# Two 128-square turns per node tile move from TensorE: the counts to transposing DMAs, the edge weights to VectorE in squares of 32 and a regrouped reload

## The reference

```python
h = relu(layernorm(x))
x1 = h @ W1 + b1                      # layer 0: 1024 -> 512, then 4 gated sums over the edges
for kk in range(4):                   #   norm = dis[src] * dis[dst], dis = max(deg, 1) ** -0.5
    out += segment_sum(norm * tanh(out[dst] @ gw[:512] + out[src] @ gw[512:] + gb) * out[src], dst)
x = x + concat([x1, out])
W = zeros(1024, 1024).at[src, dst].add(edge_weight)   # layer 1: the edge weights as a matrix
x = x + relu(layernorm(x)) @ W.T + bias
# layer 2: a GCN layer over the same edges; layer 3: an attention layer over the same edges
```

## Time and profile before

| | us |
|---|---|
| median of the runs | 975.7 |
| the profiled execution, its own time | 974.37 |
| its span, first to last instruction | 972.6 |
| TensorE busy | 955.2 |
| VectorE busy | 713.5 |
| ScalarE busy | 496.8 |
| GpSimd busy | 152.0 |

### The profile page before, as it was taken

One profiled execution on the slowest core, in us unless ns is written; L12 is line 12 of the kernel. 1 busy time (PEld: TensorE's weight loads), 2 busy tenths in 40 slices (PEclk: granted clock), 3 DMA queues, 4 the chain that ended last, 5 costly groups with the idle time before them and its releaser, 6 DMA issues.

```text
span 972.6 us, 14172 instructions
## 1 busy us (share of the span) xinstructions
PE 955.2 (98%) x5140; PEld 794.5 (82%) x5140; DVE 713.5 (73%) x1277; ACT 496.8 (51%) x768; POOL 152.0 (16%) x197
## 2 busy tenths in 40 slices
PE   5999999999999999999999999999999999999998
PEld 3888878888888888888888888888888888888887
DVE  7987798788788789558885162797856664967787
ACT  5778864554554557323334344444622323656654
POOL 3022410000000001132223000014210000333331
PEclk9999999999999999999999999999999999999999
DMA  7256491000000005453424400044952220201222
GB/s 258 88 194 230 127 209 68 0 24 0 0 22 0 0 0 119 76 172 131 129 87 126 162 1 1 1 55 116 224 126 77 82 106 0 88 22 66 86 87 82
DMA packets 28472, 83.73 MB, mean 86 GB/s; under 512 B 4696, under 2 KB 4892, under 8 KB 28272
## 3 DMA queue, kind: packets, MB, share of 16 engines
q1 hardware_dynamic: 17536, 53.48, 16.6%
q0 software_dynamic: 10880, 29.50, 12.9%
HBM read 54.65 MB, written 33.57 MB: 91 GB/s over the span
## 4 chain that ended last, share of the span: by engine, by line
PE 95%; DVE 1%; ACT 1%; DMA 1%; issue 1%; POOL 1%; SPq 0%; ACTq 0%; DVEq 0%; POOLq 0%
PE ps L659 22%; PE ps L2492 13%; PE ps L2467 10%; PE ps L2384 9%; PE ps L2386 9%; PE ps L2385 9%; PE ps L2440 5%; PE ps L2436 5%; PE ps L642 3%; PE ps L2307 2%; PE ps L2308 1%; PE ps L2309 1%; PE ps L2232 1%; PE ps L2235 1%; PE ps L2276 1%; PE ps L2503 1%
## 5 line engine op out<-in xcount | busy, mean ns | idle before, releaser
L2384 PE MATMUL ps<-g_hi,mask_hi 128*128 128x512 f32 x400 | 157.7, 394 | 0.2
L2386 PE MATMUL ps<-g_hi,mask_lo 128*128 128x512 f32 x400 | 155.9, 390 | 0.0
L2385 PE MATMUL ps<-g_lo,mask_hi 128*128 128x512 f32 x400 | 155.7, 389 | 0.0
L1232 ACT ACTIVATE mask<-ps,v 128x640 f32<-128x640 f32 x80 | 63.2, 793 | 95.7 <-PE ps L2386 49.1
L2492 PE MATMUL ps<-y_all,att_hi 128*128 128x512 f32 x380 | 103.6, 392 | 0.0
L2384 PEld LDWEIGHTS ps<-g_hi,mask_hi 128*128 128x128 f32 x400 | 75.1, 188 | 19.1 <-DVE mask_lo L1762 2.3
L2386 PEld LDWEIGHTS ps<-g_hi,mask_lo 128*128 128x128 f32 x400 | 75.1, 188 | 16.0
L2385 PEld LDWEIGHTS ps<-g_lo,mask_hi 128*128 128x128 f32 x400 | 75.1, 188 | 14.8
L2467 PE MATMUL ps<-w_hi,parts 128*128 128x512 f32 x280 | 86.7, 389 | 0.0
L659 PE MATMUL ps<-w,hT_hi 128*128 128x512 f32 x320 | 86.6, 392 | 0.0
L625 ACT ACTIVATE hT_hi<-ps 128x1024 fp32r<-128x1024 f32 x30 | 30.8, 1026 | 104.7 <-PE ps L642 104.6
(11 more groups left out here) (248 smaller groups left out, 1989.5 us busy)
## 6 DMA issues: line engine op xcount, KB each, us to landing
xin<-x_after SPq DMA_DIRECT2D x20, 512.0 KB, 3.4
x_after<-g POOLq DMA_DIRECT2D x20, 256.0 KB, 7.6
xres<-x_after POOLq DMA_DIRECT2D x10, 512.0 KB, 3.6
x_after<-xres POOLq DMA_DIRECT2D x10, 512.0 KB, 3.1
xin<-in_x SPq DMA_DIRECT2D x9, 512.0 KB, 3.7
x_after<-in_x SPq DMA_DIRECT2D x8, 512.0 KB
weight_rows<-weight_row POOLq DMA_DIRECT2D x8, 512.0 KB, 3.9
wt_raw<-weight_rows SPq DMA_DIRECT2D x4, 1024.0 KB, 20.5
```

Source lines behind the costliest of these rows:

```text
L1232: nc.scalar.activation(mask[k][:, :], U_ALL, ACT.Tanh, bias=v[:, s:s + 1]).then_inc(tanh_ready, 1)
L2384: nc.tensor.matmul(SUMS[dd], mask_hi[k][:, cols], g_hi[:, s, :], start=(s == 0), stop=False)
L2385: nc.tensor.matmul(SUMS[dd], mask_hi[k][:, cols], g_lo[:, s, :], start=False, stop=False)
L2386: last = nc.tensor.matmul(SUMS[dd], mask_lo[k][:, cols], g_hi[:, s, :], start=False, stop=(s == T - 1))
```

## The change

The counts of a tile `a` are turned by ten transposing DMAs of 128 x 128, issued from SP's queue straight from `countT` to `count_row` (`turn_counts`). SP's program reaches them three steps behind the load of `xin` (`TURN_LAG`), since the load of step `t` is issued early. ScalarE still passes over `count_row` to sum the degree (`sum_count_rows`), now in place and three groups behind the tile's last one, before two. The cast to `count_b` is gone, and so are both kinds of TensorE transposes.

The weights of a tile are turned by one VectorE instruction (`turn_weights`), which turns each square of 32 x 32 in itself. The squares then stand in the wrong place; the reload puts them right: `squares` takes 32 rows at four places, so 32 DMAs of 32 partitions with runs of 256 floats replace four DMAs of 128 partitions with runs of 1024 floats. What is left out of order is the order of the output's columns, which `residual` undoes by four instructions in place of one. The semaphore's targets follow (`Dense(1, 1, 1 + 2 * QUARTERS)`). Code for the case `whole == 0`, which these inputs do not enter, changes likewise and is left out below.

```diff
@@ -47,6 +47,7 @@
 FIRST_STEP = 2
+TURN_LAG = 3
 LATE_TILE = FIRST_STEP + 2
...
@@ -91,6 +92,9 @@
 EARLY = 3
+SQUARE = 32
+QUARTERS = P // SQUARE
+GEN_STORES = 16 * (1 + QUARTERS)
 TAIL = 3
...
@@ -378,7 +380,7 @@
-    dense = [Dense(0, 0, 1), Dense(1, 1, 2), Dense(2, 2, 4)]
+    dense = [Dense(0, 0, 1), Dense(1, 1, 1 + 2 * QUARTERS), Dense(2, 2, W2_LOAD + 1)]
...
@@ -534,6 +532,14 @@
         return bass.ds(t * P, P)
+
+    def by_quarter(row):
+
+        return row.rearrange("p (i s r) -> p s i r", i=QUARTERS, r=SQUARE)
+
+    def squares(rows_of, j):
+
+        return rows_of.rearrange("(i c) (j x) -> j c i x", c=SQUARE, j=QUARTERS)[j]
...
@@ -743,12 +749,6 @@
-    def load_weights(eng, d, dram):
-        for q in range(4):
-            eng.dma_start(W_PAIRS[d.n][q],
-                          dram[2 * q * P:(2 * q + 2) * P, :].rearrange("(k p) n -> p k n", p=P)
-                          ).then_inc(w_landed[q], 16)
-
     def settled(eng, semaphore, value):
...
@@ -762,6 +762,13 @@
             sp.dma_start(to[0:EDGE_ROWS, :, :], of.rearrange("(t p c) -> p t c", t=EDGE_TILES, c=EP)).then_inc(landed, 16)
+
+        def turn_counts(a):
+
+            sp.wait_ge(counts_copied, last_group(a) + 1)
+            sp.wait_ge(count_stored[a % 2], 16 * (a // 2))
+            for s in range(T):
+                sp.dma_start_transpose(count_row[a % 2][:, s * P:(s + 1) * P], countT[:, s, a * P:(a + 1) * P]).then_inc(count_transposed[a % 2], 16)
...
@@ -778,8 +785,15 @@
             sp.dma_start(x1_dram[(t - 2) * P:(t - 1) * P, :], x[(t - 2) * P:(t - 1) * P, :]).then_inc(rows_stored, 16)
+            for place in range(PER_STEP):
+                for a in tiles_behind(t - TURN_LAG, place, 0):
+                    turn_counts(a)
         sp.dma_start(x1_dram[(T - 2) * P:N, :], x[(T - 2) * P:N, :]).then_inc(rows_stored, 16)
         sp.dma_start(x1_dram[N:NP, :], x[0:NP - N, :]).then_inc(rows_stored, 16)
+        for t in range(T - TURN_LAG, T):
+            for place in range(PER_STEP):
+                for a in tiles_behind(t, place, 0):
+                    turn_counts(a)
...
@@ -804,7 +820,11 @@
         sp.dma_start(dis_dram.rearrange("(t p) -> p t", p=P), dis[:, 1, :], allow_slow_non_contiguous=True).then_inc(consts_landed, 16)
-        load_weights(sp, dense[1], wt_dram)
+        for q in range(4):
+            for k in (2 * q, 2 * q + 1):
+                for j in range(QUARTERS):
+                    sp.dma_start(wt_raw[SQUARE * j:SQUARE * (j + 1), k, :].rearrange("c (i x) -> c i x", i=QUARTERS),
+                                 squares(wt_dram[k * P:(k + 1) * P, :], j)).then_inc(w_landed[q], 16)
         with sp.Fori(0, GATES - 1) as r:
...
@@ -1074,17 +1092,10 @@
-        def take_weight_rows(a):
-
-            act.wait_ge(weights_transposed, a + 1)
-            act.wait_ge(weights_stored[a % 2], 16 * (a // 2))
-            nc.scalar.activation(weight_row[a % 2][:, :], ROWS, ACT.Copy).then_inc(weights_copied, 1)
-
-        def take_count_rows(a):
-
-            act.wait_ge(count_transposed, a + 1)
-            act.wait_ge(count_stored[a % 2], 16 * (a // 2))
-            nc.scalar.activation(count_row[a % 2][:, :], COUNT_ROWS, ACT.Copy,
+        def sum_count_rows(a):
+
+            act.wait_ge(count_transposed[a % 2], 16 * T * (a // 2 + 1))
+            nc.scalar.activation(count_row[a % 2][:, :], count_row[a % 2][:, :], ACT.Copy,
                                  accum_out=deg[:, a:a + 1]).then_inc(count_row_ready, 1)
...
@@ -1109,11 +1120,8 @@
                 take_cells(n)
-            for a in tiles_behind(t, place, 1):
-                if a < WT_TILES:
-                    take_weight_rows(a)
-            for a in tiles_behind(t, place, 2):
-                take_count_rows(a)
+            for a in tiles_behind(t, place, 3):
+                sum_count_rows(a)
...
@@ -1609,19 +1618,20 @@
-        def count_rows_of(a):
-
-            dve.wait_ge(counts_copied, last_group(a) + 1)
-            if a >= 2:
-                dve.wait_ge(count_transposed, a - 1)
-            nc.vector.tensor_copy(count_b[a % 2][:, :, :], countT[:, :, a * P:(a + 1) * P]).then_inc(count_b_ready, 1)
+        def turn_weights(a):
+
+            dve.wait_ge(weights_taken, min(last_group(a) + 1, WEIGHT_GROUPS))
+            dve.wait_ge(weights_stored[a % 2], 16 * (a // 2))
+            nc.vector.transpose(weight_row[a % 2][:, :].rearrange("p (j s r) -> p j s r", j=QUARTERS, r=SQUARE),
+                                weights_sd[:, :, a * P:(a + 1) * P].rearrange("p s (j c) -> p j s c", c=SQUARE)).then_inc(weights_copied, 1)
             for a in tiles_behind(t, place, 1):
-                count_rows_of(a)
+                if a < WT_TILES:
+                    turn_weights(a)
...
@@ -1844,8 +1854,10 @@
             dve.wait_ge(scale_ready, d1.norm_pairs(t // 2) + 1)
-            nc.vector.scalar_tensor_tensor(xres[b][:, :], PRODUCT[1][b], scale[:, b:b + 1], xres[b][:, :],
-                                           ALU.mult, ALU.add).then_inc(product_read[b], 1)
+            for i in range(QUARTERS):
+                there = xres[b][:, :].rearrange("p (s i r) -> p i s r", i=QUARTERS, r=SQUARE)[:, i, :, :]
+                last = nc.vector.scalar_tensor_tensor(there, by_quarter(PRODUCT[1][b])[:, :, i, :], scale[:, b:b + 1], there, ALU.mult, ALU.add)
+            last.then_inc(product_read[b], 1)
...
@@ -2240,32 +2252,10 @@
-        def weight_rows_pe(a):
-
-            pe.wait_ge(weights_taken, min(last_group(a) + 1, WEIGHT_GROUPS))
-            pe.wait_ge(count_row_ready, a)
-            for s in range(KT):
-                last = nc.tensor.transpose(ROWS[:, s * P:(s + 1) * P], weights_sd[:, s, a * P:(a + 1) * P], ident[:, :])
-            last.then_inc(weights_transposed, 1)
-
-        def count_rows_pe(a):
-
-            pe.wait_ge(count_b_ready, a + 1)
-            pe.wait_ge(weights_copied, min(a + 1, WT_TILES))
-            pe.wait_ge(count_row_ready, a)
-            for s in range(T):
-                last = nc.tensor.transpose(COUNT_ROWS[:, s * P:(s + 1) * P], count_b[a % 2][:, s, :], ident_b[:, :])
-            last.then_inc(count_transposed, 1)
-
         def place_pe(t, place):
                 cells_pe(n)
-            for a in tiles_behind(t, place, 1):
-                if a < WT_TILES:
-                    weight_rows_pe(a)
-            for a in tiles_behind(t, place, 2):
-                count_rows_pe(a)
```

More of the change, by code:

```diff
@@ L73 @@
 QK = KT // 2
-W2_LOAD = 3
+W2_LOAD = 10
 BLOCK_RING = 6
@@ L242, in build_program @@
     right = [build(f"right{k}", [P, PER_GROUP, CELLS + 3 * WCELLS], BF16) for k in range(RING)]
-    count_b = [build(f"count_b{b}", [P, T, P], BF16) for b in range(2)]
     row_ids = build("row_ids", [P, WINDOWS, 2], BF16)
@@ L795, in _ @@
                 sp.dma_start(count_dram[rows(a), :], count_row[0][:, :]).then_inc(gen_stored, 16)
-                sp.dma_start(wt_dram[rows(a), :], weight_row[0][:, :]).then_inc(gen_stored, 16)
-                settled(sp, gen_stored, 32 * (a + 1) + 1)
+                for j in range(QUARTERS):
+                    sp.dma_start(squares(wt_dram[rows(a), :], j), weight_row[0][SQUARE * j:SQUARE * (j + 1), :].rearrange("c (i x) -> c i x", i=QUARTERS)
+                                 ).then_inc(gen_stored, 16)
+                settled(sp, gen_stored, GEN_STORES * (a + 1) + 1)
         for b in range(2):
@@ L1202, in _ @@
                 for n in range(2):
-                    last = nc.scalar.activation(weight_row[0][:, n * BANK:(n + 1) * BANK], WEIGHTS[n], ACT.Copy)
+                    last = nc.scalar.activation(by_quarter(weight_row[0][:, :])[:, KT // 2 * n:KT // 2 * (n + 1), :, :],
+                                                WEIGHTS[n].rearrange("p (s i r) -> p s i r", i=QUARTERS, r=SQUARE), ACT.Copy)
                 last.then_inc(gen_copied, 1)
@@ L1526, in _ @@
     def _(dve):
-        dve.wait_ge(consts_done, 5)
+        dve.wait_ge(consts_done, 4)
         d0 = dense[0]
@@ L2181, in _ @@
     def _(pe):
-        pe.wait_ge(consts_done, 5)
+        pe.wait_ge(consts_done, 4)
         d0 = dense[0]
```

15 lines of the change are left out of this document (4 added, 11 removed).

## The result

The changed kernel takes **1057.3 us** (median of four runs, 1055.98 to 1057.66) against 975.9 us before in the same comparison: ratio 1.084, 95% interval 1.081 to 1.086. It is slower by 81 us, far outside the range of 973 to 1025. The sign was right; the size was not. The profiled execution took 1057.66 us, its span is 1055.8 us.

The account below looks back on a forecast made before the run. TensorE was taken as the bound, with other chains close behind at three places. Count chain 4.7, reload 10.1 and residual 0.4 summed to 15.2 us on 974.4, given as 990 us; range 973 to 1025, the forecast's own 982 to 1000.

Parts of the forecast that it names:

- The count chain: First stage's tail: twenty transposing DMAs at 0.6 us each delay the start of half 0 to 125.9 us, +4.7 us.
- The upper bound, 1.12 us: SP's queue: issue price from a pushed-back stretch; at it half 0 starts at 165 us, +44 us.
- 42 + 100 X + 11.2: Start of half 0 if SP's queue never catches up: counts at 42, a hundred issues, then 11.2 us to the mask.
- rival 2: First stage: transposing DMAs set the pace from about 0.8 us an issue; 1017 to 1030 us, chance 0.20.
- The estimate from the Trainium skill's page: SP's queue at 1309 ns per transposing DMA: half 0 starts at 184 us; not in the forecast sum.
- VectorE as the next bound: First stage: with turns of 1.2 us VectorE has 64.3 us of work and becomes the bound; gain 3.0 us.
- The closer wait on stored weights: First stage: a weights turn waits for stores behind counts' DMAs, 14.9 against 15.7 us; just fits at 0.6 us an issue.
- The reload: Start of half 1: 32 DMAs at 201 GB/s take 21 us instead of 10, `gw` is late, TensorE stands 10.1 us.
- The slack of 0.9 us: End of half 0: time between half 1's mask at 154.3 us and TensorE's assumed start of half 1 at 155.2.
- The rule of the Trainium skill's page: Reload: 32 partitions reach half the ports, 189 against 328 GB/s; estimated 22 us instead of 13, 9 more.
- The residual: Before the next layer: four VectorE instructions for one, nine of ten hidden in idle time; +0.4 us.
- late `gw`: Start of half 1: gate weights land 11 us late behind the reload, 0.9 us of it slack; +10.1 us.

Follow-up runs that it names:

- experiment 7: Experiment 2 with five squares of a tile by transposing DMAs and the other five moved unturned by one plain DMA: 996.5 us, ratio 1.021.
- experiment 6: Experiment 2 with each tile's ten squares stored to HBM and turned on the way back by one transposing DMA: 995.2 us, ratio 1.020.
- experiment 8: Experiment 2 with each square turned by two transposing DMAs of 64 x 128, so 200 DMAs: 1174.4 us, ratio 1.203.
- experiment 1: Changed kernel with the counts cast, turned by TensorE and copied as before, leaving only the weights part of the change: 974.4 us, ratio 0.998.
- experiment 9: Kernel before with only its reload cut into 32 DMAs of 32 partitions in runs of 1 KB, matrix layout untouched: ratio 1.006.
- experiment 10: Kernel before with only its reload cut into 32 DMAs of 32 partitions in runs of 4 KB, matrix layout untouched: ratio 1.006.
- experiment 3: Experiment 1 with the gate weights of round 1 loaded ahead of the 32 pieces of the reload: 969.8 us, ratio 0.994.
- experiment 12: Kernel before with the last three of four loads of layer 2's weights held until twenty groups of sums are done: 972.4 us, ratio 0.998.
- experiment 11: Changed kernel with the last three of four loads of layer 2's weights held until twenty groups of sums are done: 1050.7 us, ratio 1.079.
- experiment 2: Kernel before with only the counts turned by ten transposing DMAs per tile and the degree summed three groups behind: 1048.2 us, ratio 1.075.

## Why the prediction was wrong, step by step

**The count chain: the step that failed.** "I take 0.6, a little over the dearest unhindered issue" was wrong by more than a factor of two: 1.23 us is the median issue, 1.27 to 1.36 us what one costs the queue (1.48 in experiment 7). The upper bound, 1.12 us from a queue that was pushed back upon, was no bound either. The form of the reckoning held: its 42 + 100 X + 11.2 with X = 1.36 gives 189 us where 194.55 was measured; the rest is the plain DMAs in between, 6.6 us that it left out, less 1.7 us of earlier start. So the case was rival 2, named with its mark (waits for `xin` and for stored weights) and a chance of 0.20, but its price ended at 1030. The estimate from the Trainium skill's page "VectorE: DVE Perf Modes", § The three transpose paths, 184 us for the start of half 0, was nearer than any row of before: the page's 1309 ns for a 128 x 128 bf16 turn by DMA agrees with the pace of 1.27 to 1.36 us measured here on int16. But experiments 6 and 8 add that it is not a price per element: 64 x 128 holds the queue as long, and ten squares in one DMA 1.44 us. The error of method was to price a kind of DMA that the trace did not have by the nearest plain one, and then to give the far case only a fifth.

**VectorE as the next bound: right.** Said: a turn of 1.2 us, VectorE bound of the stretch, -3.0 us. Measured by the weights half alone: 1.24 us, busy 65.6 of 67 us, the stage 3.5 us shorter. That the size fits so well is partly luck, since experiment 1 keeps the ten casts (4.9 us) that the forecast took off VectorE. In the changed kernel none of it is to be seen, since the queue decides there.

**The closer wait on stored weights: right in kind.** It was said to fit at 0.6 us an issue and to fail above. At 1.36 VectorE waits 6.0 us for it, and in the weights half, without those DMAs, not at all.

**The reload: right place, wrong reason, half the size.** Said +10.1 us from a rate of 201 GB/s. Measured: a wait of 6.8 us instead of 1.0, and 5.3 us of loss in the rounds (3.8 of gap, the rest low clock). What failed is the sentence that SP's issue of 32 DMAs takes 11 us and hides under the `dis` store: it takes 25.6 us, one issue alone 5.05 (the same line's most), so `gw` is only issued at 27 us into half 0, and the reload's own rate is not what it waits for first. Experiments 9 and 10 show the cost without the regrouping. The rate itself was not far off: in experiment 3 the first issue is at 137.1 us, the last at 153.0 with 4.6 us to landing in the median, so 4.19 MB take an estimated 20.5 us, 204 GB/s. The slack of 0.9 us was misread, from the matmul of 155.17 us: from the copy behind the wait to the first matmul of half 1 it takes 234.23 - 231.44 = 2.8 us, so before, TensorE could have started half 1 at 155.4 and did so at 157.2, 1.8 us of slack. The wait is 5.8 us longer, less 1.8 leaves 4.0, near the gap of 3.8. The rule of the Trainium skill's page "SBUF — State Buffer", § Door 1: The DMA port swizzle (half the ports for 32 partitions), gave an estimated +9 us. No run here tests it: the trace has 244 GB/s at 221 to 226 us (last section), above the page's 189 for one such transfer, but here several DMAs to different partitions are in flight together, with other traffic beside them.

**The residual: right in its price, with no effect to be seen.** 1.28 us became four instructions with 1.66 us busy, +0.4, and VectorE's idle time ahead of them is still there:

```profile
L1859 DVE SCALAR_TENSOR_TENSOR xres<-ps,scale,xres 128x256 f32<-128x256 f32 x40 | 16.6, 478 | 9.5 <-DMA xres<-x_after 5.3 <-PE ps L665 3.3 <-issue 0.9
```

Without the gap in layer 2 the part behind the rounds is 566.8 us with the new residual (experiments 1 and 3) and 566.9 with the old one (experiment 12), so the 0.4 us that were to lie on the way to the next layer do not show.

**Not in the prediction**: the longer gap in layer 2 (4.5 us, experiments 11 and 12), and the clock, of which it said only that a drop would cost more than the gap. Behind the gap of half 1 the drop cost 1.7 us on top of 3.8. How much of the 73 us the low clock makes was not tried apart; as the queue is never idle until 183 us, it can add little ahead of that. Behind it the tail was 1.7 us longer than said. The first mask is ready at 193.4 us and half 0 starts at 194.55 directly behind TensorE's last products, whose first matmul, at 189.63, takes 0.77 us; their first five steps take 1.95 us where the full clock gives 1.13, so 0.8 of the 1.7 us are the low clock's.

The sum, in the terms of the prediction: count chain +73.4 (said +4.7 with 3.0 of gain spent in it; of the weights half's 3.5 the measured stage shows 0.3, 160.7 us against 161.0 in experiment 2), late `gw` +5.3 (said +10.1), everything behind the rounds, which is the gap of layer 2, +4.5 (said +0.4, for the residual): 83.2 us (said 15.2).

## What to carry to other kernels

Price a DMA by what it holds its queue for, by kind and by number, before its bytes: many small ones in a queue that also carries loads on the path pace everything behind them, the consumer engines' in-order work included. A kind of instruction that the trace does not have gets its own one-run measurement or a range wide enough for its documented price, not the price of its nearest relative. Where a change has two halves, time them apart: in the first stage one was worth -3.5 us and the other +73.6. And measure a stage from a mark at its own start: the start-up alone moved half 0 by 2.5 us between experiments 1 and 3, whose stage is the same.

## What the runs showed of the hardware

- A transposing DMA of 2-byte elements out of SBUF holds SP's queue for 1.1 us at least, 1.23 us in the median, whether it turns 64 x 128 or 128 x 128; 1280 x 128 out of HBM takes 1.44.
- A stretch in which TensorE is busy 2.9 of 20 us is granted 0.51 of the clock; it is at 1.00 again in the first 26 us of half 0. With a gap of 3.8 us at the start of half 1, the stretch of 231 to 240 us has 0.81, and the low clock in it costs 1.7 us:

```profile
195.00:221.00 26.00, 26.00 (x119) 20.96 (x118) 21.99 (x39) 16.79 (x26) 1.12 (x2) 1.00 1.22 170
221.00:226.00 5.00, 5.00 (x24) 4.12 (x23) 2.96 (x4) 3.40 (x6) 0.00 (x0) 1.00 1.14 244
...
231.00:240.00 9.00, 5.77 (x18) 4.57 (x19) 8.16 (x15) 2.58 (x4) 0.00 (x0) 0.81 0.00 1
```

- 32 plain DMAs of 128 KB cost the queue 0.51 us each some 15 us behind the `dis` store and 0.80 directly behind it, where the first alone takes 5.05, against 0.34 for a single load of 512 KB.
- With three loads of 1 MB at 400 GB/s beside it, TensorE stood still for 1.6 to 4.6 us at a place where the profile shows no wait; with the loads issued 12 to 13 us later it did not, which took 6.3 us off the part behind the rounds in one kernel (573.2 to 566.9) and 1.8 in the other (568.7 to 566.9). In two further kernels the same loads at the same place stopped nothing.
